# A six-layer local-attention stage whose loop body is folded from nine rounds to eight

## The chip, the cores and the metric

The kernel runs on one core of a Trainium2 chip. The metric is device time in microseconds (us) of one execution; less is better. The core has five engines with instruction queues of their own: PE (TensorE matmul), DVE (VectorE), ACT (ScalarE), POOL (GpSimd) and SP (SyncE, which issues most DMAs here). Semaphores order them.

## The reference, cut to what matters

Four parts follow each other: cross-attention, a mixture of attention experts, a second cross-attention, and a stack of six layers. The change is in the last part alone:

```python
for i in range(DEPTH):            # 6 layers, x is (2, 512, 128)
    x = attn_layer(shift_tokens(x), Wqkv[i], q_scale[i], k_scale[i], Wo[i]) + x
    x = ffn_layer(shift_tokens(x), ln_g[i], ln_b[i], W1[i], b1[i], W2[i], b2[i]) + x

# attn_layer: 16 heads of 64; windows of 32 keys, each query window sees its own and the one before
q = l2norm(q) * qs;  k = l2norm(k) * ksc
q = q * cos * scale + rotate_half(q) * sin * scale      # tables by position
k = k * cos / scale + rotate_half(k) * sin / scale
out = local_attention(q, k, v) @ Wo
# ffn_layer
xn = (x - mu) / sqrt(var + 1e-5) * g + bln
a, gate = split(xn @ W1 + b1)                           # 2 x 341
return a * gelu(gate, approximate=False) @ W2 + b2
```

`shift_tokens` moves half of the channels by one position, so a layer can start on a batch only when the layer before has finished that batch.

## The kernel before

The last stage is `stage_d`. The 1024 tokens are 8 tiles of 128 (`NT` = 8), four to a batch (`TB` = 4, `B` = 2). Everything is float32. The work on one tile is cut into named pieces, and `layer_order()` gives each piece a round `k` and a place `at` in it; every engine's program walks the same sorted list, and does its share of each piece. Each engine's queue is in order, so a piece that waits holds up all that stands behind it on that engine.

The pieces of tile n: `proj` in round n in four chunks of 512 columns (c = 0, 1 queries, c = 2, 3 keys; the values go with c = 0 and 2); in round n+1 the turning (PE transposes of chunk c into bank PX, ACT copy to DQT or DKT); `score`, `exp`, `weigh` in round n+2; `pturn`, `mix`, `oturn`, `out` in round n+3. The names in this text: P3.2 is the projection of tile 3, chunk 2. For each chunk, PE multiplies into PM, ACT copies to DRAW (L1487) and squares (L1496), DVE does three multiplications with the rotation tables and a sum (L1567 to L1573), POOL adds, takes the power -0.5 (L1281) and scales the keys. In `score`, PE writes 2 + 128 matmuls (L1347, L1353), DVE scales, takes the maximum and subtracts (L1579, L1582, L1584).

The feed-forward part of a batch is `f1a` (PE turns Y, ACT shifts it), `f1b` (PE turns back; DVE statistics, POOL power for RSTD, DVE normalises, L1616), `f2` (turn and scale), three times `f3` (gate and a-matmul on PE, gelu on ACT, product DU on DVE, L1627) and `f4` (24 matmuls L1444, then two additions on DVE, L1631 and L1634). It uses the banks of PM that the projections use.

A layer takes `PERIOD` = 9 rounds. Pieces with k of 9 and more are done in the rounds of the next layer (marked ' here), so that the loop body of five turns holds rounds 0 to 8; a straight piece stands ahead of it and one behind it. Round 8 has no projection, only the turning of tile 7, `score` and `exp` of tile 6, the mixing of tile 5, and the feed-forward part of batch 0:

```
round 8: score6 vin7 pturn5 P8.0 f20 P8.1 exp6 mix5 f30 P8.2 weigh6 oturn5 f31 f32 P8.3 out5 f40
round 0: early' score7' shift0 pturn6' P0.0 P0.1 exp7' mix6' P0.2 weigh7' oturn6' P0.3 out6' vout0
```

`early` (SP) loads the next layer's 1536 KB of projection weights and its scales in one go, once the last projection is done; POOL then builds the tables DTAB for all four positions from the scales (four instructions, L1269) at `shift0`.

Of the kernel before, what the change touches and what calls it, by code (L numbers as in the profile page):

```python
# [13 lines left out]
ALU = mybir.AluOpType  # L14
# [5 lines left out]
TB = S // 128  # L20
# [126 lines left out]
def bc(x, axis, shape):  # L147
    return x.unsqueeze(axis).broadcast_to(shape)
# [880 lines left out]

PERIOD = NT + 1  # L1030


def layer_order():

    forward = {(0, 0): [("f1a", None)], (0, 1): [("f1b", None)], (1, 0): [("f2", None)],
               (1, 1): [("f3", 0)], (1, 2): [("f3", 1), ("f3", 2)], (1, 3): [("f4", None)]}
    order = []  # L1040
    for k in range(NT + 5):
        s, o = k - 2, k - 3
        if k == PERIOD:
            order.append((k, -5, "early", None))
        if 0 <= s < NT:
            order.append((k, 0, "score", s))
        if 1 <= k <= NT:
            order.append((k, 5, "vin", k - 1))
        if k in (0, TB):
            order.append((k, 1, "shift", k // TB))  # L1050
        for c in range(4):
            at = 10 * (c + 1)
            if k <= NT:
                order.append((k, at, "proj", (k, c)))
            if c == 0 and 0 <= o < NT:
                order.append((k, at + -1, "pturn", o))
            if c == 1 and 0 <= s < NT:
                order.append((k, at + 1, "exp", s))
            if c == 2 and 0 <= s < NT:
                order.append((k, at + 3, "weigh", s))  # L1060
            if c in (1, 2) and 0 <= o < NT:
                order.append((k, at + 4, ("mix", "oturn")[c - 1], o))
            if c == 3 and 0 <= o < NT:
                order.append((k, at + 5, "out", o))
            for b in range(B):
                for name, x in forward.get((k - TB * (b + 1) - 3, c), []):
                    order.append((k, at + (1 if name in ("f1a", "f2") else 6), name, b if x is None else 3 * b + x))
        if k < NT:
            order.append((k, 48, "vout", k))
        if k == NT + 2:  # L1070
            order.append((k, 49, "output", None))
        if k == NT + 4:
            order.append((k, 49, "late", None))
    return order

# [28 lines left out]
def stage_d(nc, shared, d, V, out):  # L1104
    with ExitStack() as ctx:
# [25 lines left out]
        step, padded, const = m.sem("d_step"), m.sem("d_padded"), m.sem("d_const")  # L1131
        w_in, s_in = m.sem("d_w_in"), m.sem("d_s_in")
        o_in, r_in = m.sem("d_o_in"), m.sem("d_r_in")
# [5 lines left out]
        def ev(name, per, credit=0):  # L1139
            return Event(m.sem("d_" + name), per, credit)  # L1140

        tables = ev("tables", 1)

# [25 lines left out]
        with nc.Block() as block:  # L1169
            @block.sync  # L1170
            def _(sp):
                def early(i):
                    sp.dma_start(WQKV[:, :], d["WqkvR"][i].rearrange("o p n -> (o p) n")).then_inc(w_in, 16)
                    sp.dma_start(SCL[:, :, :], d["scales"][i].broadcast_to([128, 4, DL])).then_inc(s_in, 16)
# [39 lines left out]
                def piece(layer, name, n, nxt):  # L1214
                    if name == "vout":
                        vout(layer, n)
                    elif name == "vin":
                        vin(layer, n)
                    elif name == "early" and nxt is not None:
                        sp.wait_ge(pm0.filled, pm0.number(layer, ("qk", 4 * NT - 1)))  # L1220
                        sp.sem_inc(sp_passed, 1)
                        sp.wait_ge(tables.sem, tables.at(layer, 0))
                        sp.sem_inc(sp_passed, 1)
                        early(nxt)
# [9 lines left out]
                early(slice(0, 1))  # L1234
                output(slice(0, 1))
# [19 lines left out]
            def _(pool):  # L1255
# [5 lines left out]
                pool.wait_ge(const, 32)  # L1261
                pool.sem_inc(roped.sem, roped.credit)
                def piece(layer, name, n):
                    if name == "shift" and n == 0:
                        pool.wait_ge(s_in, layer * 16 + 16)
                        pool.wait_ge(rotated.sem, rotated.at(layer, -1))
                        pool.sem_inc(pool_passed, 1)
                        for i in range(4):
                            ins = g.tensor_tensor(TAB[:, i, :, :], ROT[:, i, :, :], bc(SCL[:, i, :], 1, [128, TB, DL]), ALU.mult)  # L1269
                        ins.then_inc(tables.sem, 1)  # L1270
                    elif name == "proj" and n[0] < NT:
# [28 lines left out]
            def _(pe):  # L1300
# [3 lines left out]
                def piece(layer, name, n):  # L1304
# [9 lines left out]
                    def proj(n, c):  # L1314

                        b, t = divmod(n, TB)
                        wv = WQKV[:, 2 * INNER:].rearrange("p (h r e) -> p r h e", r=2, e=DL)
# [219 lines left out]
            def _(dve):  # L1537
# [9 lines left out]
                def piece(layer, name, n):  # L1547
# [9 lines left out]
                    if name == "proj" and n[0] < NT:  # L1557
# [4 lines left out]
                        tab = TAB[:, 2 * (c // 2):2 * (c // 2) + 2, t, :]  # L1562
                        if k == 0:
                            wait(tables, 0)
                        dve.wait_ge(pm0.drained, pm0.number(layer, ("qk", k)))
# [36 lines left out]
                    elif name == "f1b":  # L1602
# [16 lines left out]
                        drained(pv, (name, n))  # L1619
# [131 lines left out]
```

## Time and profile before

| | us |
|---|---|
| median of 3 runs | 2322.89 (2321.42 to 2332.89) |
| the profiled execution, its own time | 2328.08 |
| its span, first to last instruction | 2326.2 |
| DVE busy in the span | 1716.5 |
| PE busy in the span | 1867.0 |
| last stage in the span | from 1215.9 to the end |

The span is what the trace covers; about 2 us lie around it. An engine's busy time says nothing of what it waits for: that is read from gaps in the timeline, and from who ended them. Line numbers are those of the kernel before.

### The profile page before, as it was taken

What the parts mean: (1) busy time and instruction counts of PE and PEld (TensorE: products, weight loads), DVE (VectorE), ACT (ScalarE), POOL (GpSimd) and SP (SyncE); (2) the same over time, 40 slices, a digit from 0 to 9 for tenths busy, and PEclk for the clock granted to TensorE, in tenths of its full rate; (3) what the DMA queues carried; (4) which work ended last, traced back from release to release, by engine and by line L of the source; (5) the groups of instructions that cost most, each with busy time, mean ns of one, the idle gap of its engine ahead of it and who ended that gap; (6) DMA issues with size and microseconds to landing.
All of it is one profiled execution on the core that took longest, in us unless ns stands there. A gap on an engine that the chain in (4) does not pass through costs nothing. (4 is left out here: it accounts for less than half of the span.)

```text
span 2326.2 us, 52273 instructions
## 1 busy us (share of the span) xinstructions
PE 1867.0 (80%) x18512; PEld 924.7 (40%) x18512; DVE 1716.5 (74%) x3041; ACT 1279.5 (55%) x1850; POOL 906.5 (39%) x913
## 2 busy tenths in 40 slices
PE   5745888888888888888846887887888888788786
PEld 3531222222222222222223654654655555555564
DVE  4744677767777777777648988878878887887893
ACT  4411665656666666666635655645546555555553
POOL 0012111111111111111028858648657666675670
PEclk9955898989999999999958998999999999999998
DMA  1002223232222232222004323323323333232330
GB/s 34 1 24 61 46 56 61 56 59 55 59 55 59 55 59 55 59 55 57 2 30 119 92 85 92 87 85 92 94 87 92 86 93 92 68 111 75 84 84 10
DMA packets 88745, 152.83 MB, mean 66 GB/s; under 512 B 16819, under 2 KB 51669, under 8 KB 84693
## 3 DMA queue, kind: packets, MB, share of 16 engines
q1 hardware_dynamic: 86421, 149.04, 26.2%
q8 instruction: 136, 2.23, 0.4%
q10 hardware_dynamic: 2112, 0.94, 0.2%
q14 instruction: 76, 0.62, 0.1%
HBM read 98.03 MB, written 51.12 MB: 64 GB/s over the span
## 5 line engine op out<-in xcount | busy, mean ns | idle before, releaser
L899 DVE TENSOR_REDUCE ENM<-PM 128x1 f32<-128x512 f32 x1024 | 658.4, 685 | 257.2 <-PE PM L722 248.8
L819 ACT ACTIVATE EPT<-PA 128x1024 f32<-128x1024 f32 x512 | 512.4, 1021 | 220.2 <-PE PA L734 137.6
L722 PE MATMUL PM<-EKX,EQX 48*128 48x512 bf16 x1024 | 356.3, 402 | 104.3 <-DVE ENM L899 84.0
L1279 POOL TENSOR_TENSOR DQR<-DR 128x512 f32<-128x512 f32 x192 | 245.4, 1278 | 289.0 <-DVE DR L1569 289.0
L1281 POOL TENSOR_TENSOR DRN<-DRN,DHALF 128x8 f32<-128x8 f32 x192 | 354.8, 1848 | 8.4
L642 POOL CAST ENMP<-ENM 128x16 bf16<-128x16 f32 x64 | 12.6, 196 | 786.2 <-DVE ENM L899 786.2
L744 PE MATMUL PV<-EPT,EVP 128*32 128x512 f32 x2048 | 286.7, 633 | 0.8 <-ACT EPT L819 0.7
L734 PE MATMUL PA<-EQX,EKX 51*128 51x512 bf16 x1024 | 254.8, 397 | 28.4 <-DMA EQX<-EROWS 15.9
L722 PEld LDWEIGHTS PM<-EKX,EQX 48*128 48x128 bf16 x1024 | 85.8, 95 | 482.1 <-DVE ENM L899 392.7
L1325 PE MATMUL PM<-DWQKV,DXS 128*128 128x512 f32 x384 | 218.0, 651 | 47.3 <-ACT XNT L1526 29.2
L1487 ACT ACTIVATE DRAW<-PM 128x512 f32<-128x512 f32 x192 | 114.7, 598 | 143.4 <-PE PM L1325 106.4
L1567 DVE TENSOR_TENSOR DR<-DRAW,DTAB 128x512 f32<-128x512 f32 x192 | 146.6, 764 | 37.2 <-ACT DRAW L1487 15.9
L144 PE MATMUL PA<-IDENT,DP 128*128 128x128 f32 x768 | 116.7, 293 | 46.2 <-DVE DP L1595 37.3
L144 PEld LDWEIGHTS PX<-IDENT,DQR 128*128 128x128 f32 x768 | 99.7, 147 | 111.8 <-issue 107.8
L1571 DVE TENSOR_REDUCE DSS<-DSQ 128x8 f32<-128x512 f32 x192 | 129.5, 674 | 0.0
L144 PE MATMUL PX<-IDENT,DQR 128*128 128x128 f32 x768 | 121.3, 283 | 7.6 <-issue 6.9
L144 PEld LDWEIGHTS PA<-IDENT,DP 128*128 128x128 f32 x768 | 91.1, 149 | 89.6 <-DVE DP L1595 68.5
L1496 ACT ACTIVATE DSQ<-DRAW 128x512 f32<-128x512 f32 x192 | 121.7, 634 | 0.8
L1508 ACT ACTIVATE DPT<-PA 128x512 f32<-128x512 f32 x96 | 52.3, 597 | 115.3 <-PE PA L144 113.5
L1395 PE MATMUL PV<-DWO,DOT 128*128 128x128 f32 x768 | 100.2, 286 | 15.6 <-DVE XN L1616 12.6
L1285 POOL TENSOR_TENSOR DQR<-DQR,DRN 128x512 f32<-128x512 f32 x96 | 102.0, 1063 | 13.8
L1336 PE MATMUL PM<-DWQKV,DXS 128*128 128x512 f32 x192 | 103.3, 621 | 3.3 <-DVE DU L1627 3.3
(208 smaller groups left out, 2960.9 us busy)
## 6 DMA issues: line engine op xcount, KB each, us to landing
DV<-d_vpark SPq DMA_DIRECT2D x192, 256.0 KB, 5.0
d_vpark<-DVT SPq DMA_DIRECT2D x48, 512.0 KB, 2.6
e_park<-EPARTS SPq DMA_DIRECT2D x64, 192.0 KB, 2.9
EQX<-e_park SPq DMA_DIRECT2D x32, 384.0 KB, 5.5
EKX<-e_park SPq DMA_DIRECT2D x32, 384.0 KB, 9.2
DWQKV<-in_WqkvR SPq DMA_DIRECT2D x6, 1536.0 KB, 9.5
e_park<-EPARTS SPq DMA_DIRECT2D x64, 128.0 KB, 2.7
e_park<-EPARTS SPq DMA_DIRECT2D x64, 64.0 KB, 2.1
```

The costliest lines, as they stand in the source:

```text
L144: return pe.matmul(out, lhsT=in_, rhs=m.IDENT[0:k, 0:k], is_transpose=True, start=True, stop=True)
L722: pe.matmul(PM[:, r, :], lhsT=QX[64 * r:64 * r + KQ, b, hp, t * 128:(t + 1) * 128], rhs=KX[64 * r:64 * r + KQ, b, hp, :], start=True, stop ...
L734: mm = pe.matmul(PA[:, 2 * pair + r, :], lhsT=KX[64 * r:64 * r + KS, b, hp, kt * 128:(kt + 1) * 128], rhs=QX[64 * r:64 * r + KS, b, hp, :] ...
L744: mm = pe.matmul(PV[32 * j:32 * j + 32, :], lhsT=VP[:, g // HG, kt, 4 * (g % HG) + j, :], rhs=PT[:, kt, j * S:(j + 1) * S], start=kt == 0, ...
L819: s_.activation(PT[:, kt, pair * 2 * S:(pair + 1) * 2 * S], PA[:, 2 * pair:2 * pair + 2, :].rearrange("p a b -> p (a b)"), ACT.Exp, scale= ...
L899: v.tensor_reduce(NM[:, g % 2, t, j, 0:1], PM[:, r, :], AX.X, ALU.max, negate=True).then_inc(maxed, 1)
L1279: g.tensor_tensor(qr, r1, r2, ALU.add).then_inc(roped.sem if queries else joined.sem, 1)
L1281: g.tensor_tensor(rn, rn, HALF[:, 0:8], ALU.pow).then_inc(rooted.sem, 1)
L1325: pe.matmul(PM[:, 0, :], lhsT=XS[:, b, W + t * 128:W + (t + 1) * 128], rhs=WQKV[:, c * 512:(c + 1) * 512], start=True, stop=True).then_inc ...
L1496: s.activation(SQ[:, k % 2, :], RAW[:, k % 2, :], ACT.Square).then_inc(squared.sem, 1)
L1567: v.tensor_tensor(r1, x, bc(tab[:, 0], 1, [128, 8, DL]), ALU.mult).then_inc(step, 1)
L1571: v.tensor_reduce(SS[:, k % 2, :], SQ[:, k % 2, :].rearrange("p (h e) -> p h e", h=8), AX.X, ALU.add).then_inc(summed.sem, 1)
```

## The change

The body has eight rounds (`PERIOD` = `NT`). The turning of tile 7 (P8.c) stands in round 0 of the next layer, directly ahead of P0.c; `score6`, `mix5`, `out5` go there too. `mix`, `oturn` and `out` stand ten places earlier in their round, `out` now ahead of the fourth chunk. The feed-forward part begins at the end of a round and ends with the next one (`f1a` 45, `f1b` 6, `f1c` 16, `f2` 26, first `f3` 36, rest 41 to 49); the normalisation of `f1b` on DVE is a piece of its own, `f1c`, ten places behind the statistics, and the product of `f3` on DVE is `f3v`, behind the fourth chunk. SP loads the projection weights by 512 columns, each behind the last use of its columns, in round 7; the scales come in round 1, and POOL rebuilds the table of one position in each of the rounds 5, 6, 7 and 8. The value columns of the weights are reordered on the host, so that PE reads them as one run. Eight rounds then read:

```
round 7: score5 table2 vin6 f1b0 pturn4 P7.0 weights0 mix4 f1c0 P7.1 exp5 weights1 oturn4 f20 P7.2 weigh5 weights2 out4 f30 P7.3 f3v0 f31 f3v1 weights3 f32 f3v2 vout7 f40
round 0: score6' shift0 table3' vin7' pturn5' P8.0 P0.0 mix5' P8.1 P0.1 exp6' oturn5' P8.2 P0.2 weigh6' out5' P8.3 P0.3 vout0
```

```diff
-PERIOD = NT + 1
+PERIOD = NT
...
+    for n in range(NT):
+        order += [(n, 48, "vout", n), (n + 1, 5, "vin", n)]
+        order += [(n + 2, 0, "score", n), (n + 2, 21, "exp", n), (n + 2, 33, "weigh", n)]
+        order += [(n + 3, 9, "pturn", n), (n + 3, 14, "mix", n), (n + 3, 24, "oturn", n), (n + 3, 35, "out", n)]
...
-                def early(i):
-                    sp.dma_start(WQKV[:, :], d["WqkvR"][i].rearrange("o p n -> (o p) n")).then_inc(w_in, 16)
+                def weights(i, c):
+                    for at in (c, 4 + c // 2)[0:2 - c % 2]:
+                        sp.dma_start(WQKV[:, at * 512:(at + 1) * 512], d["WqkvR"][i][:, :, at * 512:(at + 1) * 512].rearrange("o p n -> (o p) n")).then_inc(w_in[c], 16)
...
-                    elif name == "early" and nxt is not None:
-                        sp.wait_ge(pm0.filled, pm0.number(layer, ("qk", 4 * NT - 1)))
+                    elif name == "weights":
+                        sp.wait_ge(pm0.filled, pm0.number(layer, ("qk", 4 * NT - 4 + n)))
...
+                def table(t):
+                    g.tensor_tensor(TAB[:, :, t, :], ROT[:, :, t, :], SCL[:, :, :], ALU.mult).then_inc(tables.sem, 1)
...
-                            if k == 0:
-                                pe.wait_ge(w_in, layer * 16 + 16)
+                            if n == 0:
+                                pe.wait_ge(w_in[c], (layer + 1) * (16 if c % 2 else 32))
...
+                    elif name == "f1c":
                         wait(fstd, n)
...
-                    elif name == "f3":
+                    elif name == "f3v":
                         c = n % 3
```

The end of the loop body on PE (DXS is the shifted input, XN and DW the feed-forward input and weights, DWO and DOT the output projection). Before:

```order
L144 MATMUL PA<-IDENT,DP 128x128 x8
L1436 MATMUL PM<-XN,DW 128x512
L1438 MATMUL PM<-XN,DW 128x512
L1436 MATMUL PM<-XN,DW 85x512
L1438 MATMUL PM<-XN,DW 85x512
L144 MATMUL PX<-IDENT,DQR 128x128 x4
L1395 MATMUL PV<-DWO,DOT 128x128 x8
L1444 MATMUL PV<-DW,DU 128x128 x12
L1450 COMPARE_AND_BRANCH
```

Of the change (L1317 is the projection, L1387 `out`, L1428 and L1430 the gate and a-matmul, L1436 `f4`):

```order
L1387 MATMUL PV<-DWO,DOT 128x128 x8
L1428 MATMUL PM<-XN,DW 128x512
L1430 MATMUL PM<-XN,DW 128x512
L1317 MATMUL PM<-DWQKV,DXS 128x512
L144 MATMUL PX<-IDENT,DQR 128x128 x4
L1428 MATMUL PM<-XN,DW 85x512
L1430 MATMUL PM<-XN,DW 85x512
L1436 MATMUL PV<-DW,DU 128x128 x12
L1442 COMPARE_AND_BRANCH
```

`out` moved ahead of the feed-forward matmuls, and the last projection stands among them.

The same place on DVE, before:

```order
L1595 TENSOR_TENSOR DP<-PA,DREC 128x512 x2
L1627 SCALAR_TENSOR_TENSOR DU<-PM,DCOLS,XNT 128x512
L1587 TENSOR_REDUCE DSUM<-DP 128x16
L1589 RECIPROCAL DREC<-DSUM 128x16
L1627 SCALAR_TENSOR_TENSOR DU<-PM,DCOLS,XNT 85x512
L1599 TENSOR_TENSOR Y<-Y,PV 128x128
L1631 TENSOR_TENSOR Y<-Y,DB 128x512
L1634 TENSOR_TENSOR Y<-Y,PV 128x512
L1640 COMPARE_AND_BRANCH
```

Of the change (L1559 to L1565 is the chunk P7.3, L1620 the products, L1624 and L1627 the additions of `f4`):

```order
L1579 TENSOR_REDUCE DSUM<-DP 128x16
L1581 RECIPROCAL DREC<-DSUM 128x16
L1591 TENSOR_TENSOR Y<-Y,PV 128x128
L1559 TENSOR_TENSOR DR<-DRAW,DTAB 128x512
L1563 TENSOR_REDUCE DSS<-DSQ 128x8
L1565 TENSOR_SCALAR DRN<-DSS 128x8
L1620 SCALAR_TENSOR_TENSOR DU<-PM,DCOLS,XNT 128x512
L1620 SCALAR_TENSOR_TENSOR DU<-PM,DCOLS,XNT 85x512
L1624 TENSOR_TENSOR Y<-Y,DB 128x512
L1627 TENSOR_TENSOR Y<-Y,PV 128x512
L1633 COMPARE_AND_BRANCH
```

All three products now follow each other behind the fourth chunk, with no other DVE work between them and the additions.

## Rows read from the trace of the kernel before

**Rows 1.** The page: busy us, share of the span, instructions of each engine.
```profile
PE 1867.0 (80%) x18512; PEld 924.7 (40%) x18512; DVE 1716.5 (74%) x3041; ACT 1279.5 (55%) x1850; POOL 906.5 (39%) x913
```

**Rows 2.** Windows, first DRAW copy to first DRAW copy of layers 0, 1, 5.
```profile
core 0: us, PE busy (x) PEld busy (x) DVE busy (x) ACT busy (x) POOL busy (x), PEclk, DMA share, GB/s
1226.20:1386.30 160.10, 130.34 (x1905) 85.62 (x1905) 140.62 (x234) 89.29 (x157) 125.43 (x88) 0.94 0.35 95
1386.30:1567.20 180.90, 150.07 (x2137) 100.69 (x2136) 147.60 (x261) 100.23 (x173) 119.80 (x86) 0.94 0.31 88
2112.70:2326.20 213.50, 169.19 (x2362) 113.75 (x2360) 160.64 (x294) 109.77 (x185) 118.00 (x83) 0.95 0.26 69
```

**Rows 3.** Timeline of DVE, starts of score4 and score5 of layer 2.
```profile
start us, us, engine line op out<-in xcount [idle before <-releaser]
1680.90 1.22 DVE L1579 TENSOR_TENSOR DP<-PA,DRN 128x1024 f32<-128x1024 f32 x1 [0.32 <-DVE Y L1599]
1698.11 1.22 DVE L1579 TENSOR_TENSOR DP<-PA,DRN 128x1024 f32<-128x1024 f32 x1 [0.31 <-DVE Y L1599]
```

**Rows 4.** Timeline of DVE, batch 0's feed-forward part, to the next layer's first chunk.
```profile
1708.55 0.88 DVE L1605 BATCH_NORM_STATS2 ST<-PV 128x6 f32<-128x128 f32 x4
...
1711.30 1.36 DVE L1616 TENSOR_SCALAR XN<-PV,MV,RSTD 128x128 f32<-128x128 f32 x4 [1.13 <-POOL RSTD L1289]
...
1727.97 0.75 DVE L1627 SCALAR_TENSOR_TENSOR DU<-PM,DCOLS,XNT 128x512 f32<-128x512 f32 x1 [1.92 <-ACT XNT L1526]
...
1732.12 0.75 DVE L1627 SCALAR_TENSOR_TENSOR DU<-PM,DCOLS,XNT 85x512 f32<-85x512 f32 x1 [1.27 <-PE PM L1438]
1734.25 0.29 DVE L1599 TENSOR_TENSOR Y<-Y,PV 128x128 f32<-128x128 f32 x1 [1.39 <-PE PV L1395]
...
1737.58 0.69 DVE L1634 TENSOR_TENSOR Y<-Y,PV 128x512 f32<-128x512 f32 x1 [2.19 <-PE PV L1444]
1744.68 1.22 DVE L1579 TENSOR_TENSOR DP<-PA,DRN 128x1024 f32<-128x1024 f32 x1 [6.41 <-PE PA L1353]
...
1749.22 0.69 DVE L1567 TENSOR_TENSOR DR<-DRAW,DTAB 128x512 f32<-128x512 f32 x1 [0.81 <-ACT DRAW L1487]
```

**Rows 5.** Timeline of PE, `f4`, the end of the loop body, then score7'.
```profile
1734.60 2.94 PE L1444 MATMUL PV<-DW,DU 128*128 128x128 f32 x24 [0.38 <-DVE Y L1599]
1739.59 0.68 PE L1347 MATMUL PA<-DBAND,DEYE 128*128 128x512 bf16 x2 [2.05 <-issue]
...
1742.60 1.84 PE L1353 MATMUL PA<-DKT,DQT 64*32 64x64 f32 x112 [1.93 <-issue]
```

**Rows 6.** Timeline of DVE, batch 1's feed-forward part in round 3, layer 2.
```profile
1635.62 0.75 DVE L1627 SCALAR_TENSOR_TENSOR DU<-PM,DCOLS,XNT 128x512 f32<-128x512 f32 x1 [2.19 <-PE PM L1438]
...
1639.31 0.70 DVE L1567 TENSOR_TENSOR DR<-DRAW,DTAB 128x512 f32<-128x512 f32 x1 [0.92 <-ACT DRAW L1487]
```

**Rows 7.** The last layer's tail: timeline of PE, DVE and SP.
```profile
2281.52 1.09 PE L144 MATMUL PA<-IDENT,DP 128*128 128x128 f32 x8
2281.62 1.22 DVE L1579 TENSOR_TENSOR DP<-PA,DRN 128x1024 f32<-128x1024 f32 x1 [1.16 <-PE PA L1353]
...
2283.44 1.95 PE L1375 MATMUL PA<-DV,DPT 128*32 128x128 f32 x64 [0.83 <-ACT DPT L1508]
...
2287.95 2.05 PE L1395 MATMUL PV<-DWO,DOT 128*128 128x128 f32 x16 [0.69 <-ACT DOT L1512]
...
2322.56 0.41 SPq L1251 DMA_DIRECT2D out_x<-XN  x1
```

**Rows 8.** Lines L1584 and L1567 on DVE: ns min/median/max, first and last start.
```profile
L1584 DVE TENSOR_TENSOR DP<-DP,DMAX x48: 1224/1492/2065, 1257.3 to 2284.1; 128x1024 f32<-128x1024 f32 x48
L1567 DVE TENSOR_TENSOR DR<-DRAW,DTAB x192: 626/687/1676, 1228.1 to 2259.2; 128x512 f32<-128x512 f32 x192
```

**Rows 9.** Windows: round 1 of layer 2, columns as in rows 2.
```profile
1579.50:1597.70 18.20, 15.73 (x248) 10.63 (x247) 13.48 (x26) 8.68 (x17) 17.91 (x13) 0.91 0.39 103
```

**Rows 10.** The tile DWQKV: the issues and the landing of the weight load.
```profile
L1173 SPq DMA_DIRECT2D DWQKV<-in_WqkvR x6: 361/366/424, 1216.7 to 2078.6; - x6
DMA to landing us min/median/max: 7.0/9.5/9.9
```

**Rows 11.** Timeline of PE: score0 of layer 2, with no `out` ahead.
```profile
1606.84 0.59 PE L1347 MATMUL PA<-DBAND,DEYE 128*128 128x512 bf16 x2 [1.09 <-ACT DKT L1492]
```

More of the change, by code:

```diff
@@ L1026, in _ @@
                 chain.link(v.tensor_tensor(X[:, :, :], X[:, :, :], bc(BIAS[:, :], 1, [128, NT, E]), ALU.add))
-PERIOD = NT + 1
+PERIOD = NT
 def layer_order():
-    forward = {(0, 0): [("f1a", None)], (0, 1): [("f1b", None)], (1, 0): [("f2", None)],
-               (1, 1): [("f3", 0)], (1, 2): [("f3", 1), ("f3", 2)], (1, 3): [("f4", None)]}
     order = []
[L1041 to L1074, printed above, removed]
@@ new lines, in layer_order @@
+    for c in range(4):
+        for k in range(NT + 1):
+            order.append((k, 10 * (c + 1), "proj", (k, c)))
+        order.append((NT - 1, 10 * (c + 1) + 4, "weights", c))
+    for n in range(NT):
+        order += [(n, 48, "vout", n), (n + 1, 5, "vin", n)]
+        order += [(n + 2, 0, "score", n), (n + 2, 21, "exp", n), (n + 2, 33, "weigh", n)]
+        order += [(n + 3, 9, "pturn", n), (n + 3, 14, "mix", n), (n + 3, 24, "oturn", n), (n + 3, 35, "out", n)]
+    for b in range(B):
+        k = TB * b + TB + 2
+        order += [(TB * b, 1, "shift", b), (k, 45, "f1a", b), (k + 1, 6, "f1b", b), (k + 1, 16, "f1c", b), (k + 1, 26, "f2", b)]
+        for c, (at, then) in enumerate(((36, 41), (42, 43), (44, 45))):
+            order += [(k + 1, at, "f3", 3 * b + c), (k + 1, then, "f3v", 3 * b + c)]
+        order.append((k + 1, 49, "f4", b))
@@ L1079 @@
+    for t in range(TB):
+        order.append((TB + 1 + t, 2, "table", t))
+    order += [(1, 30, "scales", None), (NT + 2, 49, "output", None), (NT + 4, -1, "late", None)]
+    return sorted(order, key=lambda x: x[:2])
 FIRST = [(0, name, n) for k, at, name, n in layer_order() if k < PERIOD]
@@ L1131, in stage_d @@
         step, padded, const = m.sem("d_step"), m.sem("d_padded"), m.sem("d_const")
-        w_in, s_in = m.sem("d_w_in"), m.sem("d_s_in")
+        w_in, s_in = [m.sem(f"d_w_in{c}") for c in range(4)], m.sem("d_s_in")
         o_in, r_in = m.sem("d_o_in"), m.sem("d_r_in")
@@ L1140, in ev @@
             return Event(m.sem("d_" + name), per, credit)
-        tables = ev("tables", 1)
+        tables = ev("tables", TB)
         def bank(name, uses):
@@ L1218, in piece @@
                         vin(layer, n)
-                    elif name == "early" and nxt is not None:
-                        sp.wait_ge(pm0.filled, pm0.number(layer, ("qk", 4 * NT - 1)))
+                    elif name == "weights":
+                        sp.wait_ge(pm0.filled, pm0.number(layer, ("qk", 4 * NT - 4 + n)))
                         sp.sem_inc(sp_passed, 1)
-                        sp.wait_ge(tables.sem, tables.at(layer, 0))
+                        if n % 2 == 0:
+                            sp.wait_ge(pm1.filled, pm1.number(layer, ("v", 2 * NT - 2 + n // 2)))
+                            sp.sem_inc(sp_passed, 1)
+                        weights(slice(1, 2) if isinstance(layer, int) else bass.ds(layer + 1, 1), n)
+                    elif name == "scales":
+                        sp.wait_ge(tables.sem, tables.at(layer, TB - 1))
                         sp.sem_inc(sp_passed, 1)
-                        early(nxt)
+                        scales(slice(1, 2) if isinstance(layer, int) else bass.ds(layer + 1, 1))
                     elif name == "output" and nxt is not None:
@@ L1232, in piece @@
                         late(nxt)
-                early(slice(0, 1))
+                scales(slice(0, 1))
+                for c in range(4):
+                    weights(slice(0, 1), c)
                 output(slice(0, 1))
@@ L1262, in _ @@
                 pool.sem_inc(roped.sem, roped.credit)
-                def piece(layer, name, n):
[L1264 to L1270, printed above, removed]
+                def table(t):
+                    g.tensor_tensor(TAB[:, :, t, :], ROT[:, :, t, :], SCL[:, :, :], ALU.mult).then_inc(tables.sem, 1)
+                pool.wait_ge(s_in, 16)
+                for t in range(TB):
+                    table(t)
+                def piece(layer, name, n):
+                    if name == "table":
+                        pool.wait_ge(s_in, (layer + 1) * 16 + 16)
+                        pool.wait_ge(rotated.sem, rotated.at(layer, 4 * (TB + n) + 3))
+                        table(n)
                     elif name == "proj" and n[0] < NT:
@@ L1562, in piece @@
                         tab = TAB[:, 2 * (c // 2):2 * (c // 2) + 2, t, :]
-                        if k == 0:
-                            wait(tables, 0)
+                        if c == 0 and n[0] < TB:
+                            wait(tables, t)
                         dve.wait_ge(pm0.drained, pm0.number(layer, ("qk", k)))
@@ L1732 @@
     qs, ks = a["L1_ffn_q_scale"], a["L1_ffn_k_scale"]
[L1733 removed]
+    d["scales"] = again(np.stack([qs, swap(qs), ks, swap(ks)], 1))
     c = np.zeros((DEPTH, 128, 8), np.float32)
```

11 lines of the change are left out of this document (7 added, 4 removed).

## The prediction

> **What bounds the kernel now.** I read the page first: over the whole span PE is busy 80% and DVE 74% [rows 1]. That is a mean over stages with different limits, so I cut the last stage at the first DRAW copy of each layer and asked for windows. Layers 1 to 4 take 181.6 us each on average (2112.7 less 1386.3, by 4), and in layer 1 DVE is busy 147.6 us, PE 150.1, POOL 119.8, ACT 100.2 [rows 2]. PE's figure contains the pipelined ends of matmuls, so its real share is smaller. DVE's chain of work is what a layer cannot be shorter than as long as its work is the same: some 148 us. The question is what becomes of the other 33 us.
>
> The starts of `score` on DVE are a good clock for rounds, since it is the first piece of every full round. Between score4 and score5, a full round with no feed-forward part, they lie 17.2 us apart, with only 0.3 us idle before each [rows 3]. So a full round is DVE's own work. Where a feed-forward part stands, DVE idles: 1.1 us for POOL's RSTD, 1.9 and 1.3 for the products, 1.4 for `out5`, 2.2 for the second addition of `f4`, 6.4 for score7', and 0.8 for the next layer's first chunk [rows 4]. In round 3 the products wait 2.2 us, and P3.3 waits 0.9 [rows 6]. The 6.4 us are made on PE: 2.9 us of `f4`, then two holes in which it waits for nothing the profile shows, 2.0 us right behind the end of the loop body and 1.9 a few matmuls into it [rows 5].
>
> **What the change removes.** No DVE instruction goes: a layer has the same 32 chunks, 8 scores and 2 feed-forward parts. What goes is round 8, in which DVE has little to put between the links of the feed-forward chain, and what surrounds it: rounds 0 and 1 in which no score stands. I rebuild a layer from pieces.
>
> Eight full rounds: 8 x 17.2 = 137.6 us.
>
> Feed-forward work on DVE for a batch: statistics 0.9, normalisation 1.4, three products of 0.75, two additions of 0.7 [rows 4], and about 0.5 for two small instructions between them (my estimate): 6.4. The wait for RSTD goes: `f1c` stands behind a whole chunk and a `mix`, over 3 us of DVE work, against the 1.1 us waited now.
>
> Waits that stay, for each batch: the products now follow each other with nothing between them. The first finds its inputs ready, since its matmuls stand ahead of P7.3. The second and third each wait for a matmul that waits for the bank the product before drains: 1.3 us each, the row of the 85-row product. Then 2.2 us for `f4`. The fourth chunk stands behind the first gelu on PE and ACT; in round 3 such a chunk came 0.9 us late [rows 6], and I take that. Together 5.7.
>
> Then batch 0 alone: the next score waits over the loop's edge, 6.4 less the 0.3 that a round has anyway: 6.1. The first chunk of the next layer waits 0.8 as now and 0.9 more, because the turning of P8.0 (four transposes and an ACT copy) now stands ahead of it: 1.7. Batch 1 alone: the next score waits 1.2 us as in the tail, where no loop edge is [rows 7], less 0.3: 0.9, called 1.0.
>
> `f1a` on PE waits for DVE's `out` with only the fourth chunk left to cover both it and the score behind it. I put 0.5 us on each of the two scores: 1.0.
>
> PE's chain: the matmuls of a round take PE 14 to 15 us, and `oturn` must wait for DVE's `mix`. From a score on DVE, `mix` is done after 7.5 us; then `oturn` 0.9, the third chunk 2.2, `out` 2.0 [rows 7], the fourth chunk 1.4, an ACT copy and 2.1 of score bring PE to about 16.8, against 17.2 for DVE. That is an estimate, with 0.4 to spare; with `out` behind the fourth chunk it was more like 0.8. Holes of 1.9 us as in rows 5 would now come through more often; I add 1.0 a layer.
>
> Sum: 137.6 + 2 x (6.4 + 5.7) + 6.1 + 1.7 + 1.0 + 1.0 + 1.0 = **172.6 us a layer**, 9.0 less than now, four times: 36.0.
>
> The first layer: the stretch from score5 to the next layer's first chunk is 51.1 us now (1749.22 less 1698.11) [rows 3, 4]. After: 17.2 + 6.4 + 5.7 + 6.1, and from score6' to the chunk 4.5 + 0.9: 40.8. In it stand no longer `mix5`, `weigh6`, `out5` and `score7`, which the first layer never had to do twice; the stretch is 10.3 shorter. Rounds 0 to 6 of that layer stay as they are. With 1.0 for PE: 9.3 less.
>
> The last layer gets longer, since what was moved behind the boundary is now done with nothing beside it. Before, score7 starts 168.9 us behind the layer's first copy (2281.62 less 2112.7) [rows 2, 7]. After: 172.6 less the 4.7 from score6' to the next first copy, less 5.2 of a loop edge that isn't there, 162.7 to score6'. From there to score7: `pturn`, copy, `mix`, scaling, `oturn`, copy, `out` take 8.5 us in the tail (2281.52 to the end of the `out` at 2290.0) [rows 7], and the turning of P8.3, its copy and the score about 3.4: 12. That is 174.7, 5.8 more. Behind score7 both are the same.
>
> Total: 36.0 + 9.3 - 5.8 = **39.5 us less**. The profiled execution took 2328.08 (span 2326.2), so a like one would take 2288.6; the median of the runs shown is 5.2 lower, 2322.89, and by it the time is 2283.
>
> **What I cost at nothing.** The weights: all six pieces now follow their last use, the last one P7.3, and are needed a whole tail of feed-forward later, over 20 us; the load of the whole lands in 9.5 us, at most 9.9 [rows 10]. Without that cover each layer would pay up to 9.9. On SP they stand behind `vin6` and ahead of `vout7`; `vout7` is issued some 3 us later, and `vin7'`, behind it, is wanted by `mix7'` two rounds on. The tables: POOL's four instructions stay four, spread over four rounds; the wait for the scales on POOL goes, and it was hidden. Value columns in one run instead of 64-column pieces: the two kinds of matmul cost the same now, so nothing.
>
> DVE and POOL in each other's way: the subtraction L1584 takes 1.22 us at least and 2.07 at most, and L1567 between 0.63 and 1.68 [rows 8], long when POOL's instruction runs. The full round that I multiply has the long subtraction already; two scores that stood where POOL rested now get it, and the slow L1567 of round 1 go. I count them as even; the ends are 2 us to either side of a layer.
>
> **Rivals.**
>
> PE becomes the bound (the other side). Score n must wait until ACT has copied the keys turned in the chunk just ahead. Before, the 2.0 us of `out` lay between; now nothing does. The one score that stood so today waited 1.1 us for that copy [rows 11]. It decides from some 0.8 us a round over DVE's 17.2 (39.5 us by 48 rounds): with 1.7 more than DVE's in every round the layer is 172.6 + 13.6 = 186.2, and the kernel 2283 + 6 x 13.6 = 2365. Against it: the copy is short and DVE has a whole chunk to do meanwhile. Chance 0.08.
>
> POOL gets no rest. In round 1 it is busy 17.9 of 18.2 us, working off what round 0 left [rows 9]; before, it rested in round 8. If every round cost it 18.2, a layer would be 172.6 + 8.0 = 180.6, and with the longer tail the kernel comes to about 2325: no change. For it: POOL's share rises to 120 of 173. Against it: its mean is 15.0 us a round [rows 2], 2.2 under DVE's. With the case that the change moves waits without shortening anything: 0.10.
> The Trainium skill, page "SBUF — State Buffer", section "Who interferes with whom", says that a DVE instruction with two inputs in SBUF contends with a GpSimd instruction that reads SBUF, and one with at most one does not; the spread of L1584 and L1567 agrees, while L1579, with an input in PSUM, shows 1.22 in each row shown. By that rule alone, two more held subtractions of 0.8 us would make the layer 1.7 longer, and a POOL that never rests is where it would hurt most.
>
> The feed-forward part in 1.1 rounds exposes more: the gelu's copy chain holds P7.3 back, products wait 2.2 as in rows 6 and not 1.3. Some 4 us a layer more: 2283 + 24 = 2307. Chance 0.14.
>
> The holes at the loop's edge are partly hidden, or PE's clock, 0.94 on average in these layers [rows 2], is higher with fuller rounds: 168 us a layer, 2283 - 27 = 2256. Chance 0.16.
>
> **How the numbers follow.** My own case has 0.52 and its range is 2270 to 2298. For 8 in 10, I reach down nearly to the shorter case and up past the feed-forward case: 2260 to 2312; outside lie the slower case, most of no change and a little of the shortest. A measurement of this kernel tells changes over 0.5%, 11.6 us. Faster by more: 0.52 + 0.16 + 0.14 = 0.82; within: 0.10; slower: 0.08.
>
> **What would show it.** The windows give about 173 us a layer with DVE busy about 148. Starts of score lie 17 us apart in rounds 4 to 6 and in round 0 to 1, about 35 over the end of a layer. No wait for RSTD. Products wait 1.3 us twice in each batch. The 6.4 us at the loop's edge are still there. Score7 of the last layer starts about 12 us behind score6. I am wrong if DVE's idle time before `score` in plain rounds exceeds 1 us, with PE waiting for DKT (the first rival), or if POOL is busy all through a round (the second).

## The result, and the profile after

The kernel became slower: 2426.39 us median (2404.60 to 2436.73, 4 runs) against 2326.23 (2321.42 to 2332.89, 4 runs), a ratio of 1.042 with a 95% interval of 1.033 to 1.050. I had forecast 39.5 us less; the medians lie 100 us apart the other way, and by the ratio it is 97. The profiled execution took 2404.6 us, the shortest of the four.

One thing has to be known to read single profiles here. The stages ahead of the last one are the same code in all kernels, and yet the last stage's first load (the rotation tables) starts anywhere from 1199.7 to 1227.4 us in the fourteen profiles. So I compare kernels by their timed runs and, within profiles, by the last stage alone: from that load's issue to the end. It is 1110.3 us before and 1196.1 after: 85.8 more. That is one execution of each, and the last stage too can differ from one execution to the next.

Windows of the changed kernel, cut at the first DRAW copy of layers 0, 1, 2 and 5; columns as in [rows 2]:

```profile
1217.80:1370.60 152.80, 120.87 (x1667) 75.98 (x1667) 135.84 (x226) 84.52 (x149) 123.65 (x85) 0.94 0.37 98
1370.60:1573.40 202.80, 157.77 (x2138) 103.75 (x2136) 157.19 (x261) 100.25 (x174) 120.27 (x86) 0.92 0.29 78
1573.40:1768.60 195.20, 156.03 (x2137) 102.49 (x2136) 152.87 (x260) 100.49 (x173) 122.07 (x86) 0.92 0.31 81
2161.00:2402.70 241.70, 184.26 (x2600) 123.28 (x2598) 171.39 (x302) 115.33 (x193) 123.37 (x87) 0.94 0.25 68
```

A layer takes 197.6 us on average (2161.0 less 1370.6, by 4) against 181.6 before and 172.6 forecast. DVE's busy time, which I had taken as fixed at 148, is 152 to 157 in the four layers, 153.5 on average against 147.7 before. So of the 16.0 us that a layer grew, 5.8 are DVE's own instructions taking longer, and 10.2 are its idle time. The first layer alone got shorter, by 7.3 us; the last grew by 28.2 (241.7 against 213.5), where I had forecast 5.8.

The starts of score0 to score4 of layer 2 on DVE, to be read against [rows 3]; the feed-forward part of batch 1 lies between the second and the third row:

```profile
1608.30 1.22 DVE L1571 TENSOR_TENSOR DP<-PA,DRN 128x1024 f32<-128x1024 f32 x1 [0.41 <-PE PA L1345]
1625.87 1.22 DVE L1571 TENSOR_TENSOR DP<-PA,DRN 128x1024 f32<-128x1024 f32 x1 [0.31 <-PE PA L1345]
1659.60 1.23 DVE L1571 TENSOR_TENSOR DP<-PA,DRN 128x1024 f32<-128x1024 f32 x1 [1.32 <-PE PA L1345]
1680.44 1.21 DVE L1571 TENSOR_TENSOR DP<-PA,DRN 128x1024 f32<-128x1024 f32 x1
1700.04 1.21 DVE L1571 TENSOR_TENSOR DP<-PA,DRN 128x1024 f32<-128x1024 f32 x1
```

The last three rows bound two rounds without any feed-forward piece: 20.8 and 19.6 us, where the same rounds took 16.4 and 17.2 before. In front of the two last scores DVE does not wait at all, so the time went inside the round. In the first of these rounds DVE is busy 17.9 us against 15.9 before, in the second 18.3 against 16.6: of the 4.4 and 2.4 us more, 2.0 and 1.7 are longer DVE instructions, and the rest is waiting.

In the first of them the wait is for ACT, with the granted clock at 1.00 throughout:

```profile
1669.80 1.06 ACT L1496 ACTIVATE DP<-DP 128x1024 f32<-128x1024 f32 x1
1670.76 1.06 ACT L1504 ACTIVATE DOT<-PA 128x512 f32<-128x512 f32 x2
1671.71 0.60 ACT L1479 ACTIVATE DRAW<-PM 128x512 f32<-128x512 f32 x1
1672.34 0.69 DVE L1559 TENSOR_TENSOR DR<-DRAW,DTAB 128x512 f32<-128x512 f32 x1 [2.10 <-ACT DRAW L1479]
```

ACT does `exp`, then the copy that belongs to `oturn` (DOT), and only then the third chunk's DRAW, which DVE wants next. In the old order the chunk stands ahead of that copy. The chain of work that ended last shows a second way, in the second of these rounds (start, length, what; the mix's scaling on DVE to the next score):

```profile
1687.61 0.69 DVE DP L1587
1688.30 0.04 issue
1688.35 1.26 PE PA L144 x8
1689.60 1.53 PE PM L1317 x2
1691.14 0.85 PE PX L144 x4
1691.99 1.46 PE PM L1328 x2
1693.45 1.78 PE PV L1387 x16
1695.23 0.88 PE PM L1317 x2
...
1696.21 0.38 ACT DRAW L1479
...
1696.70 0.60 ACT DKT L1484
...
1697.53 0.59 PE PA L1339 x2
1698.12 1.41 PE PA L1345 x91
```

From the end of `mix` on DVE to the end of the score it runs on PE and ACT, through `oturn`, the third chunk (L1317, its turning, the values L1328), `out` (L1387), the fourth chunk, ACT's copy of the keys, and the score. That is the PE chain of my first rival. The score on DVE starts 0.5 us behind its end, at 1700.04, directly behind other DVE work: in this round the two chains are nearly equally long. PE's timeline gives the way in:

```profile
1684.26 0.60 PE L144 MATMUL PX<-IDENT,DQR 128*128 128x128 f32 x4
1688.35 1.26 PE L144 MATMUL PA<-IDENT,DP 128*128 128x128 f32 x8 [3.48 <-DVE DP L1587]
1689.44 1.70 PE L1317 MATMUL PM<-DWQKV,DXS 128*128 128x512 f32 x2
```

PE has the second chunk done, stands still for 3.5 us at `oturn` until DVE has scaled the mix, and the projection behind it takes 1.70 us instead of the 1.02 that it takes at full speed: the granted clock fell within this stretch from full speed to its lower level, 1.2 GHz, as two windows of it, the stop and the time behind it, show (last columns: clock, DMA share, GB/s):

```profile
1684.00:1688.00 4.00, 0.86 (x5) 0.36 (x3) 3.97 (x7) 2.55 (x4) 2.60 (x3) 1.00 0.00 0
1688.30:1692.00 3.70, 3.65 (x15) 2.41 (x16) 3.31 (x7) 1.79 (x3) 2.78 (x3) 0.68 0.00 0
```

A mean of 0.68 is a part of the stretch at the lower level and the rest at full speed. Over these layers the mean is 0.92, against 0.94 before. Over four layers DVE's wait for DRAW went from 13.4 us to the first row, and that for the score from 36.5 to the second (waited for, total, times, longest):

```profile
DVE DR L1559 <- ACT DRAW L1479: 61.3, 51, 3.1
DVE DP L1571 <- PE PA L1345: 42.5, 17, 6.8
```

### The profile page after: what moved, and what is told of

It reads as the page before. It is cut to its first block and busy times, and to the rows that moved or that the text cites. A ratio compares the mean times of both kernels' runs of the same rounds, so it can differ in the third digit from the quotient of the medians.

```text
span 2402.7 us, 52467 instructions
## 1 busy us (share of the span) xinstructions
PE 1887.7 (79%) x18512; PEld 931.6 (39%) x18512; DVE 1747.3 (73%) x3041; ACT 1280.2 (53%) x1850; POOL 919.1 (38%) x917
## 5 line engine op out<-in xcount | busy, mean ns | idle before, releaser
L1273 POOL TENSOR_TENSOR DRN<-DRN,DHALF 128x8 f32<-128x8 f32 x192 | 327.2, 1704 | 16.3
L744 PE MATMUL PV<-EPT,EVP 128*32 128x512 f32 x2048 | 281.4, 622 | 0.7 <-ACT EPT L819 0.7
L1317 PE MATMUL PM<-DWQKV,DXS 128*128 128x512 f32 x384 | 221.7, 661 | 18.4 <-ACT DRAW L1479 7.1
L1559 DVE TENSOR_TENSOR DR<-DRAW,DTAB 128x512 f32<-128x512 f32 x192 | 149.0, 776 | 97.7 <-ACT DRAW L1479 77.8
L144 PE MATMUL PA<-IDENT,DP 128*128 128x128 f32 x768 | 121.7, 301 | 64.2 <-DVE DP L1587 53.1
L1565 DVE TENSOR_SCALAR DRN<-DSS 128x8 f32<-128x8 f32 x192 | 123.9, 645 | 6.6
L1277 POOL TENSOR_TENSOR DQR<-DQR,DRN 128x512 f32<-128x512 f32 x96 | 119.8, 1248 | 14.4 <-POOL DRN L1273 1.4
L1387 PEld LDWEIGHTS PV<-DWO,DOT 128*128 128x128 f32 x768 | 93.9, 195 | 49.5 <-issue 44.9
```

The source lines that it names most:

```text
L144: return pe.matmul(out, lhsT=in_, rhs=m.IDENT[0:k, 0:k], is_transpose=True, start=True, stop=True)
L744: mm = pe.matmul(PV[32 * j:32 * j + 32, :], lhsT=VP[:, g // HG, kt, 4 * (g % HG) + j, :], rhs=PT[:, kt, j * S:(j + 1) * S], start=kt == 0, ...
L1273: g.tensor_tensor(rn, rn, HALF[:, 0:8], ALU.pow).then_inc(rooted.sem, 1)
L1559: v.tensor_tensor(r1, x, bc(tab[:, 0], 1, [128, 8, DL]), ALU.mult).then_inc(step, 1)
```

## The experiments

The kernels were run in three groups (1 to 4; 5 to 8; 9 to 12), each beside the kernel before. Line numbers of experiments 5 to 8 and 10 to 12 are one above those of the changed kernel. Theories: **P**, the changed places of `mix`, `oturn` and `out`; **C**, the feed-forward part compacted into 1.1 rounds; **F**, the fold itself (no round without projections), which fills the rounds of POOL, ACT and PE. Until experiment 5, F also stands for the parts of the change that are not order: the loads, the tables and the value columns.

**1. All three places back.** In the change:
```diff
-        order += [(n + 3, 9, "pturn", n), (n + 3, 14, "mix", n), (n + 3, 24, "oturn", n), (n + 3, 35, "out", n)]
+        order += [(n + 3, 9, "pturn", n), (n + 3, 24, "mix", n), (n + 3, 34, "oturn", n), (n + 3, 44, "out", n)]
```


> The change with three numbers undone: mix, oturn, out stand at 24, 34, 44 again instead of 14, 24, 35; everything else is as changed. Theory P (places): the changed places put PE's and ACT's wait for DVE's mix ahead of the third projection chunk, so DVE waits for DRAW in every round; then full rounds go back from about 20 to 24 us to 17 us, a layer from 196 to 172-178, and the kernel comes to 2285-2320. Theory F (fold): eight rounds with no rest round are too full for POOL, PE and ACT whatever the places are; then this stays at 2400-2430.

Measured: 2394.0 us, ratio 1.025 (1.021 to 1.030). The two plain rounds went back to 16.5 and 18.6 us on average (before 16.4 and 17.2, after 20.8 and 20.0), as P says, but the layer only to 194.4 us from score0 to score0 (before 181.2, after 196.6): the rounds with feed-forward pieces took it, 25.7 and 40.3 us from score4 to score5 and to score6 (before 17.2 and 24.0). The result lies between the two ranges given; neither P nor F alone is enough.

**2. The same three places in the kernel before** (14, 24, 35, nine rounds).

> The kernel before with those three places alone changed: mix, oturn, out at 14, 24, 35 of their round, nine rounds a layer. Theory P: full rounds grow from 17.2 to 19 us and more, 2 to 5 us in each of 8 rounds of 6 layers: 2400-2500. Theory F: no change, 2320-2335.

Measured: 2407.99 us, ratio 1.033 (1.027 to 1.039), against 2331.63: 76 us for three numbers, in the range given for P. P holds where there is no fold.

**3. and 4. Single places, in the change.** `out` to 44 alone; then `oturn` to 34 as well.
```diff
 experiment 3, in the changed kernel
-        order += [(n + 3, 9, "pturn", n), (n + 3, 14, "mix", n), (n + 3, 24, "oturn", n), (n + 3, 35, "out", n)]
+        order += [(n + 3, 9, "pturn", n), (n + 3, 14, "mix", n), (n + 3, 24, "oturn", n), (n + 3, 44, "out", n)]
 experiment 4, in experiment 3
+        order += [(n + 3, 9, "pturn", n), (n + 3, 14, "mix", n), (n + 3, 34, "oturn", n), (n + 3, 44, "out", n)]
```

> The change with out alone back at 44, so that it stands between the fourth chunk and the next score again; mix 14 and oturn 24 as changed. If the missing cover of the key copy (PE waits 1.0 us for DKT before each score) is what costs, this gives back 1 us in each of 48 rounds: 2360-2380. If oturn ahead of the third chunk is what costs, it gives little: 2400-2425. Theory F: 2400-2430.

> The change with oturn at 34 and out at 44 again, behind the third and fourth chunk; mix stays at 14. If PE's and ACT's oturn ahead of the third chunk is the cause, this gives back nearly all that a_all_back does: within 10 us of it. If the early mix is, it stays near a_out_back. Theory F: 2400-2430.

Measured: 2467.21 (ratio 1.058, 1.054 to 1.063) and 2433.47 (1.044, 1.038 to 1.050). Both expectations failed: giving `out` back made the change slower (1.058 against 1.042), and `oturn` with it left it where it was (1.044). `out` at 44 stands directly ahead of `f1a` at 45, which on PE waits for what DVE makes of `out`: 9.1 us in four layers of the changed kernel, 23.6 in experiment 3, 33.8 in experiment 4. That is a part of the loss only. In experiment 1, too, PE waits at the two places where it meets DVE's feed-forward work (PE waited for; four layers; L1593 is the signal behind `out`'s addition, ahead of `f1a`; L1613 that behind `f1c`, ahead of `f2`):

```profile
PE PV L144 <- DVEq L1593: 26.5, 8, 3.9
PE PV L144 <- DVEq L1613: 23.4, 8, 3.0
```

So places cannot be judged one by one in this order, and I went on from the changed code with the old order in it.

**5. The changed code, old order.** Nine rounds; weights by 512 columns, tables by position and value columns as changed.

```diff
-PERIOD = NT
+PERIOD = NT + 1
-            k = TB * b + TB + 2
+            k = TB * b + TB + 3
+        order += [(k, 11, "f1a", b), (k, 26, "f1b", b), (k, 26.1, "f1c", b), (k + 1, 11, "f2", b)]
+        for c, at in enumerate((26, 36, 36.2)):
+            order += [(k + 1, at, "f3", 3 * b + c), (k + 1, at + 0.1, "f3v", 3 * b + c)]
+        order.append((k + 1, 46, "f4", b))
```


> The changed code with the order of before in it: nine rounds, mix, oturn, out and the feed-forward pieces where they stood, f1c directly behind f1b and each f3v directly behind its f3. What is left of the change is the weights by 512 columns, the tables by position, and the reordered value columns. If these cost nothing: 2315-2335. If they share in the loss (a table or a weight that comes late, POOL's queue): above 2345.

Measured: 2330.27 us, ratio 1.0025 (0.9999 to 1.0052). The new loads, tables and value columns together cost nothing that can be told from zero, as predicted. Round by round it is not nothing: score3 to score4, the round at whose start POOL now makes the first table, is 18.6 us here as in experiment 1, against 17.2 before, while the rounds at the layer's end are about 0.5 shorter. So up to 1.4 of the 2.8 us that this round has grown by in the changed kernel go with the table and not with the places. The pieces of the weights land in 2.6 to 5.4 us each in the changed kernel's trace.

**6. `f1c` one chunk later** in experiment 5.
```diff
-        order += [(k, 11, "f1a", b), (k, 26, "f1b", b), (k, 26.1, "f1c", b), (k + 1, 11, "f2", b)]
+        order += [(k, 11, "f1a", b), (k, 26, "f1b", b), (k, 32, "f1c", b), (k + 1, 11, "f2", b)]
```

> As c9, with f1c one chunk behind f1b (place 32 instead of 26). My prediction's step that the wait for RSTD goes away (13.8 us in four layers, 3.4 a layer): then 18-20 us under c9. If DVE just waits elsewhere for the same thing, no difference.

Measured: 2310.07 us, ratio 0.994 (0.992 to 0.997): 20 us under experiment 5 in the same group, as expected. In the one profile of each the last stage is 10.7 us shorter (1104.8 against 1115.5), and the same code ahead of it 13.2 us, so how much of the 20 us is the wait stays open. DVE's wait for RSTD, four layers:

```profile
DVE XN L1610 <- POOL RSTD L1282: 16.1, 9, 2.3
```
in experiment 5, and here
```profile
DVE XN L1610 <- POOL RSTD L1282: 0.8, 5, 0.2
```

**7. The compact feed-forward part in nine rounds.** In experiment 5, with `out` at 44:
```diff
-        order += [(k, 11, "f1a", b), (k, 26, "f1b", b), (k, 26.1, "f1c", b), (k + 1, 11, "f2", b)]
-        for c, at in enumerate((26, 36, 36.2)):
-            order += [(k + 1, at, "f3", 3 * b + c), (k + 1, at + 0.1, "f3v", 3 * b + c)]
-        order.append((k + 1, 46, "f4", b))
+        order += [(k - 1, 45, "f1a", b), (k, 6, "f1b", b), (k, 16, "f1c", b), (k, 26, "f2", b)]
+        for c, (at, then) in enumerate(((36, 41), (42, 43), (44, 46))):
+            order += [(k, at, "f3", 3 * b + c), (k, then, "f3v", 3 * b + c)]
+        order.append((k, 49, "f4", b))
```

> As c9, nine rounds, but the feed-forward part of a batch in 1.1 rounds as in the change (f1a 45, f1b 6, f1c 16, f2 26, first f3 36, rest 41 to 49), with mix and oturn at their old places and out at 44. Theory C (compact): PE's queue is in order, and f1a and f2 stand so close behind the DVE work they wait for that PE stops and DVE then waits for PE; then this is slower than c9 by 5 us a batch or more, 2370 and above. Theory F (the fold alone): as c9, or faster, since round 8 is then free of it.

Measured: 2389.81 us, ratio 1.028 (1.024 to 1.033), 60 over experiment 5. C holds, in the size expected. PE now stops at both meeting points in every batch, and DVE's wait for the score behind them is 83.5 us in four layers, where experiment 5 has 41.1:

```profile
PE PV L144 <- DVEq L1594: 13.7, 8, 2.8
PE PV L144 <- DVEq L1614: 13.3, 8, 3.8
DVE DP L1572 <- PE PA L1346: 83.5, 26, 7.1
```

And it has nearly the order of experiment 1 in nine rounds: 2389.8 and 2394.0, 192.8 and 194.4 us a layer. Between these two stands hardly more than the fold, and in this order it gives nothing and costs little. Against F.

**8. and 9. The feed-forward part spread, eight rounds.** Places of mix, oturn, out 24, 34, 45.

```diff
 experiment 8 (k is the round of the next score)
+        order += [(k, 1, "f1a", b), (k, 11, "f1b", b), (k, 22, "f1c", b), (k, 31, "f2", b)]
 experiment 9
+        order += [(k, 1, "f1a", b), (k, 8, "f1b", b), (k, 16, "f1c", b), (k, 31, "f2", b)]
+        order += [(k, 36, "f3", 3 * b), (k, 38, "f3v", 3 * b), (k, 42, "f3", 3 * b + 1), (k, 43, "f3v", 3 * b + 1)]
+        order += [(k, 46, "f3", 3 * b + 2), (k, 47, "f3v", 3 * b + 2), (k, 49, "f4", b)]
```


> Eight rounds, mix 24, oturn 34, out 45 as before, and the feed-forward part later: f1a behind the next round's score (1), f1b 11, f1c 22, f2 31, first f3 36, rest as in the change. Theory C: PE no longer stops at f1a and less at f2, so 5 us a batch come back against a_all_back (2394): 2320-2350. Theory F: as a_all_back or slower.

> Eight rounds as a8_late (2360), with the feed-forward part spread further: f1b 8, f1c 16 (a chunk and a mix more between it and f2 at 31), the first product ahead of the fourth chunk, out between the second and third. If what a fold costs is only that DVE and PE stand in turn at the feed-forward pieces: 10 to 30 us under a8_late, 2330-2350. If the fold has a floor: 2355-2370.

Measured: 2360.43 us (1.015, 1.010 to 1.020), a little over the range given, and 2317.44 us (0.997, 0.993 to 0.9997), under it. In experiment 8 PE's stop at `f1a` fell to 4.6 us in four layers, that at `f2` was still there:

```profile
PE PV L144 <- DVEq L1614: 26.5, 8, 3.5
PE PV L144 <- DVEq L1594: 4.6, 6, 0.9
```

In experiment 9 the stop at `f1a` is 4.4 us, that at `f2` is not among PE's waits, and the layer is 180.3 us. So eight rounds have no floor above nine. They come out level with the kernel before: 0.3% under it, with an interval that only just leaves out zero.

**10. and 11. `out`, and `mix` with `oturn`, alone in nine rounds.** In experiment 5:
```diff
-        order += [(n + 3, 9, "pturn", n), (n + 3, 24, "mix", n), (n + 3, 34, "oturn", n), (n + 3, 45, "out", n)]
 experiment 10
+        order += [(n + 3, 9, "pturn", n), (n + 3, 24, "mix", n), (n + 3, 34, "oturn", n), (n + 3, 38, "out", n)]
 experiment 11
+        order += [(n + 3, 9, "pturn", n), (n + 3, 14, "mix", n), (n + 3, 24, "oturn", n), (n + 3, 45, "out", n)]
```

> As c9 (nine rounds, 2330), with out alone moved ahead of the fourth chunk (38), oturn and mix as before. This is the rival I gave 0.08: nothing lies between the fourth chunk and the next score, so PE waits some 1.0 us for the copy of the keys. If that is the cost: 1 us in each of 48 rounds, 2370-2385. If DVE's chunk covers it: 2325-2340.

> As c9, with mix at 14 and oturn at 24 (ahead of the second and the third chunk), out as before. If oturn ahead of the third chunk on PE and ACT, waiting for DVE's mix, is the cost of the changed places (b_early: 76 us): 2380-2410. If it takes out as well: 2330-2350.

Measured: 2437.32 us (1.046, 1.040 to 1.053) and 2414.67 (1.038, 1.032 to 1.044). The second is 5 us over the range that P gave. The first is twice what I gave the missing cover. PE's waits in it, four layers:

```profile
PE PA L1340 <- ACT DKT L1485: 24.4, 24, 1.1
PE PM L1318 <- ACT XNT L1519: 23.4, 4, 5.9
PE PV L1388 <- ACT DOT L1505: 20.9, 20, 1.6
```

Experiment 5 has the second of these too, 23.4 us; the other two are 5.4 and 1.3 there. The 1.0 us for the keys is there in most rounds, and `out` itself, now directly behind `oturn`, waits 1.0 us for ACT's copy of it. In the old order the fourth chunk lies between `oturn` and `out` and covers that copy, and `out` lies between the chunk and the score and covers the copy of the keys. One swap removes both covers. The two waits grew by 9.7 us a layer, where the layer grew by 19; the granted clock is 0.90 against 0.93 to 0.94 in experiment 5, and the rest was not taken apart.

DVE's busy time tells the two apart: per layer it is 148.7 us in experiment 5, 149.6 with `out` moved and 155.8 with `mix` and `oturn` moved. So `out` costs by waiting, and of the 13 us a layer that `mix` and `oturn` cost, 7 are longer DVE instructions.

**12. `f3` earlier** in experiment 6, so that `weigh` lies between two of its products.
```diff
-        for c, at in enumerate((26, 36, 36.2)):
+        for c, at in enumerate((24.5, 31, 36)):
```

> As c9_split (nine rounds, 2310), with the second f3 one piece earlier (31), so that weigh lies between its product and the next: fills one of the two 1.3 us waits a batch. 5 to 15 us under c9_split: 2295-2305. If the waits only move: 2305-2315.

Measured: 2313.27 us, ratio 0.994 (0.992 to 0.997). That is the second of the cases given: against experiment 6 (0.994, another group) no difference can be told; its last stage is the shortest of all in one profile, 1096.5 us.

## Why the prediction was wrong, step by step

**What bounds the kernel.** "So a full round is DVE's own work" was the reading that failed. DVE has no visible wait in a plain round of the old order, but for the new order PE's chain was nearly as long in my own text: 16.8 against 17.2. Nor did those two numbers belong together. The 7.5 us from a score to the end of `mix` fit a subtraction of 1.22 us; in the round whose 17.2 I took it lasted 2.06:

```profile
1683.41 2.06 DVE L1584 TENSOR_TENSOR DP<-DP,DMAX 128x1024 f32<-128x1024 f32 x1
```

With that, PE's chain is some 17.6 us by my own terms, and longer than DVE's round. In the changed kernel's round shown above it is 19.1 us from the score at 1680.44 to the end of the next one on PE: `mix` done after 7.9 (7.5 in the prediction), `oturn` 1.3 (0.9), the third chunk 3.8 (2.2), `out` 1.8 (2.0), the fourth chunk 1.5 (1.4), ACT's copy 0.8, the score 2.0 (2.1). The third chunk was mis-sized most, since it ran at the lower clock behind PE's stop.

**Eight full rounds of 17.2.** This term failed. I took the length of a round from the old order and used it for a new one, in which three of its pieces had moved. Those places alone cost 76 us in nine rounds (experiment 2), where I had allowed 1.0 us a layer. Not all rounds grew: from one score to the next, score0 first, the means of four layers are 17.9, 34.6, 20.8, 20.0, 23.9, 38.4, 23.4 and 17.7 us. The mechanism stood in the text, as the rival with 0.08. What I had priced wrong: only the wait for the keys, not that `oturn` ahead of the third chunk makes PE and ACT stand at a piece that waits for DVE, with DVE's next input behind it. My sign for that rival, more than 1 us of idle time before `score` in plain rounds, did not come: the time went into DRAW and into DVE's own instructions. And the one wait of 1.1 us that I took from [rows 11] is score1's and not score0's; score0 had no `out` ahead either and did not wait.

**The feed-forward waits.** I gave batch 1 13.1 us above two plain rounds, of them 6.4 of DVE's work; it took 18.1 (score0 to score2, less 2 x 17.2). With the compact order 60 us were lost in nine rounds (experiment 7), some 10 a layer. I had counted DVE's waits one by one and not PE's: PE stops at `f1a` and `f2`, some 3 us each in experiment 1 and 1.7 in experiment 7, and what stands behind them, the next score and chunks, comes late. I had called `f1a` 0.5. The waits that I did count came out near: products 6.8 us a layer (5.2 forecast), second additions 5.0 (4.4).

Places alone cost 76 us and the compact part alone 60, but both with the fold some 100: the losses overlap, and how much belongs to each hangs on which is undone first. Undone in the changed kernel, the places give back some 1.6% (ratios 1.042 and 1.025), under 40 us.

**The fold.** Forecast: the main gain. Experiments 1 and 7 differ in hardly more than it and come out within 4 us. The work is the same, and round 8 was not idle: 23.5 us before, with the feed-forward part in it. In experiment 7, where that part stands elsewhere, it is 16.7. There score5 to the next layer's score0 takes 84.8 us, in experiment 1 without round 8 78.4; but score0 to score5 takes 116.0 instead of 108.0. What the end of the layer gains, the other rounds pay.

**The RSTD wait.** Right, by experiment 6: the wait fell from 16.1 to 0.8 us in four layers, and the kernel by 20 us as timed, 10.7 by its last stage in one pair of profiles. In the changed kernel it is gone too. Before, it was 13.8 us in four layers, 3.4 a layer.

**What was costed at nothing.** Right for the weights, tables and value columns together (experiment 5). Not for POOL and DVE in each other's way: after, DVE is busy 3 to 10 us a layer longer with the same instructions, 5.8 on average. The small instruction that floors the sums grew most (page of the changed kernel; busy, mean ns, idle before):

```profile
L1565 DVE TENSOR_SCALAR DRN<-DSS 128x8 f32<-128x8 f32 x192 | 123.9, 645 | 6.6
```

It takes 0.17 us at least and some 0.74 at the median, 0.65 on average and 0.49 before. Over the four layers that is 6.2 us a layer more, a little over DVE's whole growth; other instructions grew and shrank by less. What decides is POOL's instruction at that moment. Two pairs, the first from the changed kernel, the second from the kernel before:

```profile
1673.79 1.27 POOL L1271 TENSOR_TENSOR DQR<-DR 128x512 f32<-128x512 f32 x1 [1.81 <-DVE DR L1561]
1674.34 0.74 DVE L1565 TENSOR_SCALAR DRN<-DSS 128x8 f32<-128x8 f32 x1
1671.01 2.03 POOL L1281 TENSOR_TENSOR DRN<-DRN,DHALF 128x8 f32<-128x8 f32 x1
1672.83 0.17 DVE L1573 TENSOR_SCALAR DRN<-DSS 128x8 f32<-128x8 f32 x1
```

Every one over 0.3 us began while POOL was in one of its two instructions on 128x512, and ended within 0.04 us of that instruction's end: 71 of 71 in four layers before, 113 of 113 after. The 57 others before and 10 of the 15 others after began while POOL took the power (128x8), and were not held up. The Trainium skill, page "SBUF — State Buffer", section "Who interferes with whom", counts tensor_scalar among the operations that can take the port pair shared with GpSimd, so that one waits for the other's whole instruction. The trace agrees for POOL's two large instructions and not for the power (57 of 57 not held up before). No run here takes POOL away, so that it is this port is argued and not shown. In the prediction I told that section's rule for DVE instructions with one input without its exception for the two-port modes, and so did not look at this small instruction at all.

Why the two meet more often can be read as well. POOL waits for a chunk's products on DVE, in four layers before and after (waited for, total, times, longest):

```profile
POOL DQR L1279 <- DVE DR L1569: 220.4, 54, 23.8
POOL DQR L1271 <- DVE DR L1561: 253.6, 102, 21.3
```

Where POOL has caught up, its instruction on 128x512 starts right behind the products, and the small DVE instruction, 0.6 us later, falls into it. Where POOL is behind, it is mostly in the power at that moment (57 of 74 before). In the changed kernel POOL has caught up at 102 of 128 chunks instead of 54; experiment 11, with `mix` and `oturn` alone earlier, has 102 and experiment 5 has 58. So POOL does not fall behind; it keeps up, and that is when it is in the way. That the chunks lie further apart on DVE in the new order, and POOL catches up by it, is my reading of this. Over all kernels DVE is busy 149 to 157 us a layer where `mix`, `oturn` or `out` stood at a changed place, and 145 to 149 where all three stood at old ones or `out` one place off, so this goes with the places and not with the fold.

**The loop's edge.** Right: 6.7 us before score6' (1762.53), 6.4 before. The next layer's first chunk then waits 3.1 us, where I gave 1.7.

**The tail.** The last layer is 28.2 us longer, forecast 5.8. Most of it is the same longer rounds: score6 starts 182.4 us behind the layer's first copy, forecast 162.7. Then score7 stands 15.3 us behind score6 (2343.44 to 2358.76), forecast 12; in experiments 1, 8 and 9 it is 11.4, and behind score7 all kernels take some 44 us. The estimate was near for an order in which `out` follows the chunk.

**POOL without rest.** It did not happen: POOL's busy time stays 120 to 122 us a layer, in layers that grew to 197.6.

## What to carry to other kernels

A round that shows one engine without gaps may still have a second chain almost as long, and an edit of the order can move that chain first. Both chains have to be measured in the same round. Before a round's length is used for a new order, every piece that moves is followed on each in-order queue: what it waits for, what stood between the two as cover, and what is now held up behind it. Here the order was best where a consumer stood a whole piece behind its producer on every engine (experiments 6 and 9 against 5 and 8), and folding a round away gave nothing, since the spacing of the pieces was what hid their latency. And an instruction's own length is not fixed by its shape: it has to be asked what the neighbouring engine does at that moment.

## What the runs showed of the hardware that I had not expected

A stop of PE can cost twice: behind the 3.5 us stop shown above the matmuls ran at the lower clock, 1.70 us for a projection that takes 1.02, and in the slowest order tried (experiment 3) the mean granted clock of four layers was 0.89 against 0.94. A DVE instruction on 128x8 took 0.17 us or some 0.74, by which instruction POOL was in when it began. The same code ahead of the last stage differed by 28 us between profiles, which a study of 1% effects has to take out.
